# Key gathers cut in four and value loads in two, with seven instead of six score groups ahead of the next exponent pass

## The chip, the cores and the metric

The kernel runs on one core of a Trainium2 chip, in one launch. The metric is the device time in microseconds. Three runs of the kernel before gave 947.57, 948.26 and 948.73 us; the median is 948.26 us.

## The reference, cut to what matters

The reference is a two-layer perceiver block on a sequence of 128 queries of width 256. Each layer is a cross attention to a context of 12544 rows, a second mixer (a gated delta net in layer 0, a linear attention with decay in layer 1) and a mixture of experts. The change touches only the cross attention of layer 1:

```
q = (layernorm(x) @ Wq.T + bq).reshape(128, 16 heads, 16)      # 128 queries
k = (ctx @ Wk.T + bk).reshape(12544, 16 heads, 16)
v = (ctx @ Wv.T + bv).reshape(12544, 16 heads, 16)
scores = einsum('qhd,khd->hqk', q, k) / 4
out = einsum('hqk,khd->qhd', softmax(scores), v)               # the mask is all ones
x = x + out
```

## The kernel before, in words

The context is walked in 14 chunks (NCH) of 896 columns (CH), a chunk being 7 tiles of 128. Layer 0's attention is computed first, and in its passes over the chunks the kernel also makes layer 1's keys (split in three bf16 terms, laid out as 96 rows per head) and values, and stores them in DRAM: `kscr[0]` holds the first 512 columns of each chunk, `kscr[1]` the other 384, and `vscr` the values. Between the layers stand the delta net and the first mixture of experts. From about 549 us on, layer 1's attention reads all of that back.

**The loads.** `gather(sp, c, half)` (L1595) issues one DMA of 96 rows: 16 KB a row for half 0 (1536 KB), 12 KB a row for half 1 (1152 KB). `fetch_values(sp, c)` (L1601) issues one DMA of 128 rows of 8036 bytes (1004.5 KB). Both go into rings of three buffers (R1 = 3) and all are issued by SyncE, in the order of `second_sync` (L1692): in each turn of its loop half 1's gather for chunk c+2, the values of c+2, the three small DMAs of `rows(c+1)` (L1697) and half 0's gather for c+3. After the first turn this reads, in time: `rows(c+1)`, then gathers of half 0 and half 1 of chunk c+3 back to back, then the values.

**The online softmax.** A chunk is worked on twice. First come the maxima: for each head h, "S h" of the plan is one pair of matmuls (`score`, L1810, matmuls at L1818: 128x512 and 128x384) into one of two pairs of PSUM banks, and one VectorE reduction over 896 columns (`largest`, L1974). A pair of banks is free again when the reduction two places before has read it. After S15 VectorE updates the running maximum (L1989), GpSimd turns it into three bf16 terms (`maximum`, L1747: L1750 to L1762), TensorE transposes them ("M", L1826), ScalarE copies them out (L2026), and `rows` moves them by DMA into three rows of the tile `home` (`qrows`), so that the next score matmuls yield the score minus the maximum. The second pass over the chunk has 28 units: TensorE's transposed scores for four heads and one tile (`scores`, L1861, four matmuls, in pairs of units: "x8"), ScalarE's exponent of 128x512 (L2035), and TensorE's product with the values (`values`, L1874, 16 matmuls a unit, four units in a row: the profile shows "x32" pieces with the weights' passes). "R" (L1835, L1994) turns a finished chunk's output and adds it.

**The order.** The order of all engines is written out by hand. Unit groups of the second pass run in 7 x 3 slots (t = 0 to 6, k = 0 to 2): slots k = 0 and 1 hold two score units each, slot k = 2 holds the four value units of the tile. After each slot come the entries of `PLAN1[t][k]` (L1656). `SPLIT = 6` says that S0 to S5 of the plan belong to chunk c+2 and S6 to S15 to chunk c+1. `PRO1` is what is done ahead of the first unit: all S of chunk 0, S0 to S2 of chunk 1, M of chunk 0, then S3 to S5 of chunk 1. TensorE executes strictly in this order. "Chunk c" below means the turn in which the second pass of chunk c is done; one such turn is called a period.

**The waits that matter.** `score` waits at h = 0 for the chunk's two gathers (L1815). `turn_maximum` waits for GpSimd's last term. `scores` waits at u = 0 for `rows` (L1854). `score` also waits, by `sm_free` (L1798), for the reduction two places before.

Of the kernel before, what the change touches and what calls it, by code (L numbers as in the profile page):

```python
# [20 lines left out]
ALU = mybir.AluOpType  # L21
# [7 lines left out]
CT = 7  # L29
CH = CT * P  # L30
HT = (4, 3)
# [10 lines left out]
S0 = D0 ** -0.5  # L42
H1, D1 = 16, 16
# [5 lines left out]
KROWS = NJ * D1  # L49
# [17 lines left out]
def build(nc, a, out):  # L67
# [4 lines left out]
    def S(name):  # L72

        if name not in sems:
            sems[name] = nc.alloc_semaphore(name)
        return sems[name]
# [11 lines left out]
    def some(value):  # L88

        return not (isinstance(value, int) and value <= 0)  # L90
# [24 lines left out]
    with ctx:  # L115
# [14 lines left out]
        half = sb(keep, "half", [P, 2])  # L130
# [128 lines left out]
        kscr = [nc.dram_tensor(f"kscr{half}", (NCH, NJ, P, DC, HW[half]), BF16).ap() for half in range(2)]  # L259
        vscr = nc.dram_tensor("vscr", (NCH, P, CT, VW), F32).ap()  # L260
# [589 lines left out]
        R = sb(gd, "R", [P, NH, P])  # L850
# [9 lines left out]
        w = sq  # L860
# [731 lines left out]
        pickhome = v1[:, 2].rearrange("p t w -> p (t w)")[:, 0:3 * HB * KROWS // 2]  # L1592
        picks = pickhome.bitcast(BF16).rearrange("p (l k r) -> p l k r", l=HB, k=3)

        def gather(sp, c, half):  # L1595

            sp.dma_start(krows[half][0:KROWS, c % R1].rearrange("r h m -> r (h m)"),
                         kscr[half][c].rearrange("j (d h) b m -> (j d) (h b m)", d=D1)
                         ).then_inc(S(f"krows{half}_{c % R1}"), 16)

        def fetch_values(sp, c):  # L1601

            sp.dma_start(v1[:, c % R1].rearrange("p t w -> p (t w)"),
                         vscr[c].rearrange("p t w -> p (t w)")).then_inc(S(f"v1_{c % R1}"), 16)

        def l1_loads(sp):
            o = (0, 6, 8, 10)
# [19 lines left out]
        def value_ones(pool, r):  # L1627
# [21 lines left out]
        LB = (6, 7, 0, 1, 2)  # L1649
        UNITS = CT * H1 // GH  # L1650
        SLOTS = 3
        SPLIT = 6

        PLAN1 = (  # L1656
            (("S6",), ("S7",), ("R",)),
            (("S8",), ("S9",), ("S10",)),
            (("S11",), ("S12",), ("S13",)),
            (("S14",), ("S15",), ("S0",)),  # L1660
            (("S1",), ("M",), ("S2",)),
            (("S3",), ("S4",), ()),
            (("S5",), (), ()))

        def plan1(c, t, k):

# [79 lines left out]
        def second_gpsimd(pool):  # L1746
            def maximum(c):  # L1747
                s = c % 2
                pool.wait_ge(S("run1"), c + 1)
                pool.tensor_scalar(neg1[:], run1[:, s], -1.0, None, ALU.mult).then_inc(S("maxstep1"), 1)  # L1750
                if some(c):
                    pool.wait_ge(S("mt1"), c)
                pool.tensor_scalar(n31[:, 0, 0:H1], run1[:, s], -1.0, None, ALU.mult).then_inc(S("maxstep1"), 1)
                if some(c - 1):
                    pool.wait_ge(S("f1"), c - 1)
                pool.tensor_tensor(dm1[:, s], run1[:, 1 - s], run1[:, s], ALU.subtract).then_inc(S("dm1"), 1)
                pool.wait_ge(S("maxstep1"), 4 * c + 2)
                pool.tensor_tensor(neg1[:], neg1[:], n31[:, 0, 0:H1], ALU.subtract).then_inc(S("maxstep1"), 1)
                pool.wait_ge(S("maxstep1"), 4 * c + 3)
                pool.tensor_copy(n31[:, 1, 0:H1], neg1[:]).then_inc(S("maxstep1"), 1)  # L1760
                pool.wait_ge(S("maxstep1"), 4 * c + 4)
                pool.tensor_tensor(n31[:, 2, 0:H1], neg1[:], n31[:, 1, 0:H1], ALU.subtract).then_inc(S("n31"), 1)  # L1762

            def rescale(c):
                pool.wait_ge(S("acc1"), 2 * c + 1)
                pool.wait_ge(S("f1"), c + 1)
                pool.tensor_tensor(acc1[:], acc1[:], bc(f1[:, c % 2, :], 2, [P, H1, D1 + 1]), ALU.mult).then_inc(S("acc1"), 1)

            def block_mask():
                pool.memset(blk16[:], 1.0).then_inc(S("blk16"), 1)  # L1770
                pool.wait_ge(S("blk16"), nth("blk16"))
                v = blk16[:].rearrange("p (b u) -> p b u", u=DL)
                pool.affine_select(out=v, in_=v, compare_op=ALU.is_ge, fill=0.0, base=0,
                                              pattern=[[-DL, P // DL], [0, DL]], channel_multiplier=1).then_inc(S("blk16"), 1)
                pool.wait_ge(S("blk16"), nth("blk16"))
                pool.affine_select(out=v, in_=v, compare_op=ALU.is_ge, fill=0.0, base=DL - 1,
                                              pattern=[[DL, P // DL], [0, DL]], channel_multiplier=-1).then_inc(S("blk16"), 1)

            make_picks(pool)
            ln_pool(pool, "ln2")  # L1780
            pool.wait_ge(S("qpick_psum"), NPICK)
            value_ones(pool, 2)
            pool.wait_ge(S("v1late_ones"), 4)
            pool.wait_ge(S("q3"), 3)
            for half in range(2):
                pool.memset(krows[half][KROWS:KONES].rearrange("p s h m -> p (s h m)").bitcast(F32),  # L1786
                            TWO_ONES).then_inc(S("krows_ones"), 1)
                pool.wait_ge(S("krows_ones"), half + 1)
            for c in range(NCH):
                maximum(c)  # L1790
                if c:
                    rescale(c - 1)
                else:
                    block_mask()
            rescale(NCH - 1)

        def second_tensor(pe):
# [12 lines left out]
            def score(c, h):  # L1810

                r, b = c % R1, sm_bank(("S", c, h))
                if h == 0:
                    for half in range(2):
                        pe.wait_ge(S(f"krows{half}_{r}"), 16 * (c // R1 + 1))  # L1815
                sm_free(("S", c, h))
                for half in range(2):
                    ins = pe.matmul(bank[b + half][:, 0:HW[half]], qrows[0:KROWS, 0, h, :],  # L1818
                                    krows[half][0:KROWS, r, krow(h), :], start=True, stop=True)
                ins.then_inc(S("sm1"), 1)  # L1820
# [44 lines left out]
            def values(c, u):  # L1865
                t, j, g = u // 4, u % 4, UNITS * c + u
                pe.wait_ge(S("exp1"), g + 1)
                if u == 0:
                    if some(c):
                        pe.wait_ge(S("ots1"), c)  # L1870
                    pe.wait_ge(S(f"v1_{c % R1}"), 16 * (c // R1 + 1))
                for i in range(GH):
                    h = GH * j + i
                    ins = pe.matmul(bank[OT1][32 * i:32 * i + 32, j * P:(j + 1) * P],  # L1874
                                    v1[:, c % R1, t, h * (D1 + 1):h * (D1 + 1) + 32],
                                    p1[:, g % PR, i * P:(i + 1) * P],
                                    start=(u == 0), stop=(t == CT - 1), skip_group_check=True)
                ins.then_inc(S("pv1"), 1)
# [403 lines left out]
```

## Time and profile before

| what | value |
|---|---|
| median of three runs | 948.26 us |
| the profiled execution's own time | 944.76 us |
| its span (first to last instruction) | 943.0 us |
| TensorE busy | 899.3 us, 95% of the span |
| VectorE, ScalarE, GpSimd busy | 704.8, 487.5 and 300.1 us |
| granted TensorE clock, mean | 0.989 |
| layer 1's attention, second pass over 14 chunks | about 596.5 to 906 us |

The profiled execution lies 3.5 us under the median of the timed runs (0.37%), so only differences are carried from one to the other. The rows further down come from the profile page of this execution and from questions put to its trace; times in them are microseconds from the start of the span.

### The profile page before, as it was taken

To read this page: it belongs to the slowest core of one execution; us is meant where nothing else is said; L and a number is where in the kernel's file an instruction comes from. 1 tells how busy PE (TensorE), PEld (TensorE's weight loads), DVE (VectorE), ACT (ScalarE), POOL (GpSimd) and SP (SyncE) were. 2 spreads that over 40 slices of the span, in tenths; PEclk is the share of its full clock that TensorE was granted. 3 is DMA by queue.
4 is the path that set the end of the run, shared out by engine and by line. 5 is a ranking of instruction groups with operands and counts; after the bars stand their busy time and mean duration, and the time that the engine had idled before them with its cause. 6 is when DMAs were issued, how large, how long until landed. Compare 5 with 4: busy or idle time off the path is not lost. (4 is left out here: it accounts for less than half of the span.)

```text
span 943.0 us, 21457 instructions
## 1 busy us (share of the span) xinstructions
PE 899.3 (95%) x8230; PEld 580.0 (62%) x8230; DVE 704.8 (75%) x1216; ACT 487.5 (52%) x1156; POOL 300.1 (32%) x435
## 2 busy tenths in 40 slices
PE   8999999999999999999999989989999999999987
PEld 5444554455445545567788856666667666776675
DVE  3499888988898889997577448768778788887426
ACT  2543454345434544344583413556667666666742
POOL 5564346434643464445065127201100000000100
PEclk9999999999999999999999979999999999999999
DMA  9467855575356535533300078786666667766000
GB/s 171 171 185 211 250 183 171 143 186 183 104 143 186 180 103 158 132 117 119 134 1 1 1 186 215 203 210 163 163 164 164 163 176 185 177 180 187 5 3 6
DMA packets 103655, 136.33 MB, mean 145 GB/s; under 512 B 64152, under 2 KB 85424, under 8 KB 100880
## 3 DMA queue, kind: packets, MB, share of 16 engines
q1 hardware_dynamic: 99856, 134.22, 52.3%
q10 hardware_dynamic: 3712, 0.92, 0.6%
q8 instruction: 59, 0.97, 0.4%
q14 instruction: 28, 0.23, 0.1%
HBM read 81.48 MB, written 53.07 MB: 143 GB/s over the span
## 5 line engine op out<-in xcount | busy, mean ns | idle before, releaser
L1974 DVE TENSOR_REDUCE mx<-bank 128x1 f32<-128x896 f32 x224 | 232.9, 1086 | 54.6 <-PE bank L1818 53.1
L2035 ACT ACTIVATE p<-bank 128x512 f32<-128x512 f32 x392 | 202.9, 602 | 103.7 <-PE bank L1861 103.4
L704 DVE STREAM_TRANSPOSE ew<-sc 32x896 f32<-32x896 f32 x208 | 229.3, 1102 | 15.3 <-ACT sc L788 7.7
L563 PE MATMUL bank<-Wv,ctxT 128*128 128x512 f32 (+1 forms) x336 | 146.4, 575 | 0.0
L1861 PE MATMUL bank<-home,krows 99*128 99x128 bf16 x1568 | 124.7, 220 | 7.7 <-issue 3.4
L1861 PEld LDWEIGHTS bank<-home,krows 99*128 99x128 bf16 x1568 | 101.3, 98 | 46.4 <-issue 9.9
L1818 PE MATMUL bank<-krows,home 96*128 96x512 bf16 x448 | 123.0, 355 | 1.7 <-DMA krows<-kscr 0.9
L1874 PE MATMUL bank<-p,v 128*32 128x128 f32 x3136 | 108.0, 276 | 3.2 <-issue 3.1
L563 PEld LDWEIGHTS bank<-Wv,ctxT 128*128 128x128 f32 x336 | 63.6, 190 | 71.6 <-issue 64.1
L1874 PEld LDWEIGHTS bank<-p,v 128*32 128x32 f32 x3136 | 80.8, 110 | 31.3 <-ACT p L2035 23.0
L445 POOL CAST kt<-kf 128x512 bf16<-128x512 f32 (+1 forms) x56 | 31.3, 558 | 203.3 <-ACT kf L760 203.3
L1750 POOL TENSOR_SCALAR neg<-run 128x16 f32<-128x16 f32 x14 | 3.6, 256 | 264.8 <-DVE run L1989 264.7
L543 PE MATMUL bank<-ctxT,WTk 128*128 128x512 f32 (+1 forms) x192 | 82.5, 552 | 0.7 <-ACT WTq L752 0.7
L760 ACT ACTIVATE kf<-bank,b 128x512 f32<-128x512 f32 (+1 forms) x56 | 35.5, 635 | 87.6 <-PE bank L543 86.5
L527 PE MATMUL bank<-ctxT,Wk 128*128 128x448 f32 x192 | 76.9, 545 | 1.3 <-DVE ctxT L317 1.3
L788 ACT ACTIVATE sc<-sc,neg 128x448 f32<-128x448 f32 x112 | 74.4, 667 | 0.0
L651 DVE CUSTOM_DVE_ANT_0 sc<-bank,pen 128x448 f32<-128x448 f32 x112 | 63.9, 621 | 4.8 <-issue 4.6
L775 ACT COPY v<-bank 128x256 f32<-128x256 f32 x77 | 28.7, 373 | 66.9 <-PE bank L563 66.9
L748 ACT COPY kT<-bank 128x448 f32<-128x448 f32 x56 | 29.8, 532 | 61.9 <-PE bank L527 61.9
L543 PEld LDWEIGHTS bank<-ctxT,WTk 128*128 128x128 f32 x192 | 34.5, 189 | 44.4 <-issue 37.0
L451 POOL TENSOR_TENSOR kt<-kf,kt 128x512 bf16<-128x512 f32 (+1 forms) x56 | 58.2, 1039 | 4.4
L447 POOL TENSOR_TENSOR kt<-kf,kt 128x512 bf16<-128x512 f32 (+1 forms) x56 | 58.0, 1036 | 4.5
(317 smaller groups left out, 1158.1 us busy)
## 6 DMA issues: line engine op xcount, KB each, us to landing
krows<-kscr SPq DMA_DIRECT2D x14, 1536.0 KB, 9.9
krows<-kscr SPq DMA_DIRECT2D x14, 1152.0 KB, 14.7
v<-vscr SPq DMA_DIRECT2D x14, 1004.5 KB, 13.8
vscr<-vpair SPq DMA_DIRECT2D x12, 1004.5 KB, 4.0
kscr<-kt SPq DMA_DIRECT2D x14, 768.0 KB, 3.6
kscr<-kt SPq DMA_DIRECT2D x14, 576.0 KB, 5.1
kscr<-kt SPq DMA_DIRECT2D x14, 512.0 KB, 4.5
ctxB<-ctx SPq DMA_DIRECT2D x56, 112.0 KB, 4.0
```

Source lines behind the costliest of these rows:

```text
L451: pool.tensor_tensor(kh[:, 2, b], f, kh[:, 1, b], ALU.subtract).then_inc(S("k31"), 1)
L527: ins = pe.matmul(bank[kv_bank(op, s)][:, 0:HCH], Wk0[:, i, b * P:(b + 1) * P], turned_context(c)[:, i, half * HCH:(half + 1) * HCH], star ...
L543: ins = pe.matmul(bank[kv_bank(op, s)][:, 0:HW[half]], WTk[:, i, b * P:(b + 1) * P], turned_context(c)[:, i, HO[half]:HO[half] + HW[half]] ...
L563: ins = pe.matmul(bank[kv_bank(op, s)][:, 0:w * D], turned_context(c)[:, i, k * P:(k + 1) * P], Wv01[:, i, 0:w].rearrange("p w o -> p (w o)"),
L651: dve.tensor_tensor_reduce(out=sc0[:, s, h, half * HCH:(half + 1) * HCH], in0=bank[SX[k % 4]][:, 0:HCH], in1=pen0[:, half * HCH:(half + 1) ...
L704: dve.transpose(pT0[j * SQ:(j + 1) * SQ, :, :, i * SQ:(i + 1) * SQ].rearrange("m t h q -> m h t q"), rows[:, j]).then_inc(S("turn0"), 1)
L788: act.activation(sc0[:, s, h, cols], sc0[:, s, h, cols], ACT.Exp, bias=neg0[:, h:h + 1], accum_out=den0[:, s, h, half:half + 1]).then_inc( ...
L1818: ins = pe.matmul(bank[b + half][:, 0:HW[half]], qrows[0:KROWS, 0, h, :], krows[half][0:KROWS, r, krow(h), :], start=True, stop=True)
L1861: ins = pe.matmul(bank[ST1[g % 3]][:, i * P:(i + 1) * P], krows[half][:, c % R1, krow(h), cols], qrows[:, c % 2, h, :], start=True, stop=True)
L1874: ins = pe.matmul(bank[OT1][32 * i:32 * i + 32, j * P:(j + 1) * P], v1[:, c % R1, t, h * (D1 + 1):h * (D1 + 1) + 32], p1[:, g % PR, i * P: ...
L1974: dve.tensor_reduce(mx1[:, c % 2, h:h + 1], psum[:, b:b + 2, :].rearrange("p b n -> p (b n)")[:, 0:CH], AX.X, ALU.max).then_inc(S("smread1 ...
L2035: act.activation(p1[:, g % PR, :], bank[ST1[g % 3]][:], ACT.Exp).then_inc(S("exp1"), 1)
```

## The change

It has four parts.

1. `gather` issues four DMAs in place of one, each for a quarter of the row's 16 head blocks: 4 KB a row for half 0, 3 KB for half 1. All count on the same semaphore, and `score` waits for all four (16 * GPARTS).
2. `fetch_values` issues two DMAs in place of one: tiles 0 to 3 (4592 bytes a row) and 4 to 6 (3444 bytes). `values` waits for both.
3. `SPLIT` is 7, and `PLAN1` is shifted by one: S6 moves from the first slot of a chunk to slot k = 1 of its last tile (there for chunk c+2), every later S moves up one place, and the slot behind the value units of tile 3 becomes empty. `PRO1` gains one S of chunk 1.
4. In `maximum` GpSimd's subtraction `dm1`, which the rescaling factor needs, moves behind the three steps that M waits for.

```diff
+        GPARTS = 4
+
         def gather(sp, c, half):
-            sp.dma_start(krows[half][0:KROWS, c % R1].rearrange("r h m -> r (h m)"),
-                         kscr[half][c].rearrange("j (d h) b m -> (j d) (h b m)", d=D1)
-                         ).then_inc(S(f"krows{half}_{c % R1}"), 16)
+            for part in range(GPARTS):
+                heads = slice(part * H1 // GPARTS, (part + 1) * H1 // GPARTS)
+                sp.dma_start(krows[half][0:KROWS, c % R1, heads].rearrange("r h m -> r (h m)"),
+                             kscr[half][c].rearrange("j (d h) b m -> (j d) (h b) m", d=D1)[:, heads].rearrange("r h m -> r (h m)")
+                             ).then_inc(S(f"krows{half}_{c % R1}"), 16)
 
         def fetch_values(sp, c):
-            sp.dma_start(v1[:, c % R1].rearrange("p t w -> p (t w)"),
-                         vscr[c].rearrange("p t w -> p (t w)")).then_inc(S(f"v1_{c % R1}"), 16)
+            for tiles in (slice(0, HT[0]), slice(HT[0], CT)):
+                sp.dma_start(v1[:, c % R1, tiles].rearrange("p t w -> p (t w)"),
+                             vscr[c, :, tiles].rearrange("p t w -> p (t w)")).then_inc(S(f"v1_{c % R1}"), 16)
...
-        SPLIT = 6
+        SPLIT = 7
         PLAN1 = (
-            (("S6",), ("S7",), ("R",)),
-            (("S8",), ("S9",), ("S10",)),
-            (("S11",), ("S12",), ("S13",)),
-            (("S14",), ("S15",), ("S0",)),
+            (("S7",), ("S8",), ("R",)),
+            (("S9",), ("S10",), ("S11",)),
+            (("S12",), ("S13",), ("S14",)),
+            (("S15",), ("S0",), ()),
             (("S1",), ("M",), ("S2",)),
             (("S3",), ("S4",), ()),
-            (("S5",), (), ()))
+            (("S5",), ("S6",), ()))
...
                 pool.tensor_scalar(n31[:, 0, 0:H1], run1[:, s], -1.0, None, ALU.mult).then_inc(S("maxstep1"), 1)
-                if some(c - 1):
-                    pool.wait_ge(S("f1"), c - 1)
-                pool.tensor_tensor(dm1[:, s], run1[:, 1 - s], run1[:, s], ALU.subtract).then_inc(S("dm1"), 1)
...
                 pool.tensor_tensor(n31[:, 2, 0:H1], neg1[:], n31[:, 1, 0:H1], ALU.subtract).then_inc(S("n31"), 1)
+                if some(c - 1):
+                    pool.wait_ge(S("f1"), c - 1)
+                pool.tensor_tensor(dm1[:, s], run1[:, 1 - s], run1[:, s], ALU.subtract).then_inc(S("dm1"), 1)
...
-                        pe.wait_ge(S(f"krows{half}_{r}"), 16 * (c // R1 + 1))
+                        pe.wait_ge(S(f"krows{half}_{r}"), 16 * GPARTS * (c // R1 + 1))
...
-                    pe.wait_ge(S(f"v1_{c % R1}"), 16 * (c // R1 + 1))
+                    pe.wait_ge(S(f"v1_{c % R1}"), 32 * (c // R1 + 1))
```

On TensorE the change moves the S pairs against the other groups. The place is the third and fourth tile of a chunk up to M, in the kernel before: the pair in the fourth and fifth row is S14, the next one S15, the one behind the value group (L1874) S0 of the next but one chunk, then S1.

```order
L1874 MATMUL bank<-p1,v1 32x128 x16
L1861 MATMUL bank<-home,krows1 128x128 x8
L1818 MATMUL bank<-krows0,home 128x512
L1818 MATMUL bank<-krows1,home 128x384
L1874 MATMUL bank<-p1,v1 32x128 x16
L1818 MATMUL bank<-krows0,home 128x512
L1818 MATMUL bank<-krows1,home 128x384
L1861 MATMUL bank<-home,krows1 128x128 x8
L1818 MATMUL bank<-krows0,home 128x512
L1818 MATMUL bank<-krows1,home 128x384
L1861 MATMUL bank<-home,krows1 128x128 x8
L1826 MATMUL bank<-identb,n31 96x128
```

And now (L1823 is the score, L1866 the transposed scores, L1879 the values, L1831 is M), from the same place on:

```order
L1866 MATMUL bank<-home,krows1 128x128 x8
L1823 MATMUL bank<-krows0,home 128x512
L1823 MATMUL bank<-krows1,home 128x384
L1866 MATMUL bank<-home,krows1 128x128 x8
L1823 MATMUL bank<-krows0,home 128x512
L1823 MATMUL bank<-krows1,home 128x384
L1879 MATMUL bank<-p1,v1 32x128 x16
L1866 MATMUL bank<-home,krows1 128x128 x8
L1823 MATMUL bank<-krows0,home 128x512
L1823 MATMUL bank<-krows1,home 128x384
L1866 MATMUL bank<-home,krows1 128x128 x8
L1831 MATMUL bank<-identb,n31 96x128
```

No S pair stands any more behind that value group: the last pair ahead of it, which was S15, is now S0, and S15 is the pair before. On SyncE, one turn of the loop before (`home<-n3T` is `rows`):

```order
L1697 DMA home<-n3T 1x16x128 x3
L1597 DMA krows<-kscr 96x8192
L1597 DMA krows<-kscr 96x6144
L1603 DMA v<-vscr 128x2009
L1697 DMA home<-n3T 1x16x128 x3
```

And one turn now:

```order
L1702 DMA home<-n3T 1x16x128 x3
L1601 DMA krows<-kscr 96x2048 x4
L1601 DMA krows<-kscr 96x1536 x4
L1608 DMA v<-vscr 128x1148
L1608 DMA v<-vscr 128x861
L1702 DMA home<-n3T 1x16x128 x3
```

The order of the three kinds is kept; ten DMAs of the large tiles stand where three stood.

## Rows read from the trace of the kernel before

**Rows 1.** The page: busy us, share of the span, instructions, by engine.

```profile
PE 899.3 (95%) x8230; PEld 580.0 (62%) x8230; DVE 704.8 (75%) x1216; ACT 487.5 (52%) x1156; POOL 300.1 (32%) x435
```

**Rows 2.** Whom TensorE waited for, 597 to 908 us (total, times, longest).

```profile
PE bank L1826 <- POOL n L1762: 3.9, 11, 0.7
PE bank L1861 <- issue: 3.4, 3, 2.4
PE bank L1874 <- issue: 3.1, 3, 1.5
...
PE bank L1861 <- DMA home<-n3T: 1.1, 2, 0.8
```

**Rows 3.** Instructions in time, 791 to 796 us (start, duration, engine, line).

```profile
791.00 0.55 PE L1818 MATMUL bank<-krows,home 96*128 96x512 bf16 x2
...
792.49 0.55 PE L1818 MATMUL bank<-krows,home 96*128 96x512 bf16 x2
...
793.66 0.22 POOL L1756 TENSOR_TENSOR dm<-run 128x16 f32<-128x16 f32 x1
...
794.41 0.22 POOL L1762 TENSOR_TENSOR n<-neg,n 128x16 bf16<-128x16 f32 x1
...
794.68 0.26 PE L1826 MATMUL bank<-identb,n 128*96 128x128 bf16 x1 [0.33 <-POOL n L1762]
...
795.23 0.28 ACT L2026 COPY n3T<-bank 96x128 bf16<-96x128 bf16 x1
...
795.54 1.93 SPq L1697 DMA_DIRECT2D home<-n3T  x3
```

**Rows 4.** The same view, one period on.

```profile
816.30 0.26 PE L1826 MATMUL bank<-identb,n 128*96 128x128 bf16 x1 [0.32 <-POOL n L1762]
```

**Rows 5.** M in all chunks (ns min/median/max, first and last start).

```profile
L1826 PE MATMUL bank<-identb,n x14: 227/257/257, 592.8 to 883.9; 128*96 128x128 bf16 x14
```

**Rows 6.** SyncE in time, 795.5 to 797.6 us.

```profile
797.51 0.59 SPq L1597 DMA_DIRECT2D krows<-kscr  x1
```

**Rows 7.** The page: DMA issues (count, KB, median us from issue to landing).

```profile
krows<-kscr SPq DMA_DIRECT2D x14, 1536.0 KB, 9.9
krows<-kscr SPq DMA_DIRECT2D x14, 1152.0 KB, 14.7
```

**Rows 8.** DMA issues, 774 to 779.4 us (the same columns).

```profile
krows<-kscr SPq DMA_DIRECT2D x1, 1152.0 KB, 13.8
```

**Rows 9.** DMA issues, 730.5 to 731 us.

```profile
krows<-kscr SPq DMA_DIRECT2D x1, 1152.0 KB, 15.2
```

**Rows 10.** Busy time in stretches; last figures clock, DMA share, GB/s.

```profile
777.00:784.00 7.00, 7.00 (x125) 5.46 (x126) 5.00 (x7) 5.07 (x10) 0.00 (x0) 1.00 1.05 246
...
790.00:791.00 1.00, 1.00 (x16) 0.73 (x13) 1.00 (x2) 0.93 (x2) 0.00 (x0) 1.00 1.00 418
```

**Rows 11.** DMA queues, 731 to 738.8 us (packets, MB, share).

```profile
q1 hardware_dynamic: 134, 1.84, 99.3%
```

**Rows 12.** DMA queues, 738.8 to 739 us.

```profile
q8 instruction: 1, 0.02, 37.5%
```

**Rows 13.** TensorE in time, 738.5 to 742.5 us.

```profile
738.96 1.07 PE L1874 MATMUL bank<-p,v 128*32 128x128 f32 x31
741.58 0.30 PE L1874 MATMUL bank<-p,v 128*32 128x128 f32 x1 [1.55 <-issue]
```

**Rows 14.** TensorE in time, the first pass and its start, 566 to 600 us.

```profile
570.24 0.54 PE L1818 MATMUL bank<-krows,home 96*128 96x512 bf16 x2 [0.88 <-DMA krows<-kscr]
...
592.79 0.26 PE L1826 MATMUL bank<-identb,n 128*96 128x128 bf16 x1 [1.11 <-POOL n L1762]
...
596.51 0.83 PE L1861 MATMUL bank<-home,krows 99*128 99x128 bf16 x12
```

**Rows 15.** The boundary of the first two chunks, 606 to 623 us.

```profile
613.58 1.78 SPq L1697 DMA_DIRECT2D home<-n3T  x3
...
619.59 1.01 PE L1861 MATMUL bank<-home,krows 99*128 99x128 bf16 x8 [2.36 <-issue]
```

## The prediction

> **What bounds the kernel now.** I read the page first: TensorE is busy 899.3 of 943.0 us [rows 1], so whatever is gained must be idle time of TensorE or work that stands in its way. The change lies in layer 1's attention alone, so next came the list of whom TensorE waited for between 597 and 908 us [rows 2]. It is short. Eleven waits for GpSimd's last term ahead of M sum to 3.9 us; six waits with the releaser "issue", behind which the profile shows nothing, sum to 6.5 us; two for the small DMAs of `rows` sum to 1.1 us. M is run 14 times from 592.8 to 883.9 us [rows 5], so a period takes (883.9 - 592.8) / 13 = 22.4 us on average, or 22.2 us without the one wait of 2.36 us at the first boundary [rows 15]. A period with no such gap, from M at 794.68 to M at 816.30, takes 21.6 us [rows 3, 4]. It holds one wait of 0.33 us at M, so TensorE's own work in a period is 21.3 us.
>
> **The wait at M.** In time around 794 us [rows 3]: GpSimd's last term starts at 794.41 and M follows at 794.68, 0.33 us later than TensorE could have come. ScalarE copies M out at 795.23 and SyncE issues `rows` at 795.54. Part 3 brings S15 one S place forward, and the reductions go at VectorE's pace of one S place, about 1 us; part 4 takes one GpSimd step of 0.22 us [rows 3] out of the chain. Both together exceed the 0.33 us by far: the wait at M goes in all periods. ScalarE's copy, however, stands behind four exponents in its own order that wait for TensorE's scores, so `rows` is not issued earlier relative to the scores.
>
> **The gaps with "issue".** At 740.03 TensorE stops for 1.55 us in the middle of a value group [rows 13]. The DMA queues give the reason. Queue q8 carries only instructions, in packets of 16 KB. From 731 to 738.8 us there is no such packet, while the gathers' queue keeps the DMA engines 99% busy [rows 11]; then, at 738.8 to 739 us, one appears [rows 12], just when half 0's gather (issued at about 730, median 9.9 us to landing, rows 7) is through, and TensorE goes on 2.6 us after it. I read this as a fetch of TensorE's own instructions that had to stand behind a whole gather. With a quarter of the gather in each DMA, it would stand behind a quarter: the gather's share of each engine is six rows of 16 KB now, about 7 us at 246 GB/s in sum (1573 KB / 246 = 6.4 us, rows 10), and 1.6 us afterwards.
>
> The Trainium skill ("DMA: Bandwidth & Descriptors", section "Queues, rings and completion order") says that a DMA engine alternates between its queues and finishes what it has as one packet before it switches. The trace agrees as far as the late fetch at 738.8 goes; nothing in it shows a fetch beside small transfers.
>
> So parts 1 and 2 may return most of 6.5 - 2.4 = 4.1 us (the 2.36 us gap of rows 15 is another matter, below), and part 3 another 3.9. If nothing else came in, each period would fall to 21.3 us.
>
> **What is late next: the gathers.** Part 3 also moves S0 of chunk c+3 forward, from 792.49 to the place where S15 stood, 791.00 [rows 3]: the value group between them is now behind it. S0 waits for both gathers of its chunk. Those are issued behind `rows`. This closes a loop that has nothing to do with TensorE's load:
> - from the first of `rows` to the issue of the second gather, which follows the first at once: 797.51 + 0.59 - 795.54 = 2.6 us [rows 3, 6];
> - from there to the landing of half 1: median 14.7 us [rows 7], 13.8 in one period and 15.2 in another [rows 8, 9];
> - from S0's new place to the next `rows`: 795.54 - 791.00 = 4.5 us [rows 3].
>
> The sum is 21.8 us (20.9 to 22.3). Before, with S0 at 792.49, the last piece is 3.05 us, the sum is 20.3, and the loop is hidden under 22.2. Afterwards it is longer than TensorE's 21.3 us. So I expect TensorE to wait at S0 for the gathers, and a period to take 21.8 us.
>
> **Do the quarters land sooner or later?** The trace has no such transfer. From above: SyncE issues six more, and if each cost the 0.59 us of one issue [rows 6] in sequence, landing would come 3.5 us later and a period would take 25.3 us. From below: the values alone move at 418 GB/s against the gathers' 246 [rows 10]; the 2688 KB of both (2.75 MB) take 6.6 us at that rate, not 11.2, and then the loop is well under 21.3. I take no change, which is nearest to the rows: the queue is never empty behind the first quarter (393 KB take 1.6 us, an issue takes 0.6), and bytes and rows are the same.
>
> The skill's same page (section "Bandwidth") has a rule against this change: batch DMAs to at least 1 MiB, a transfer of 64 KB being mostly overhead. By its table a transfer of a few hundred KB runs under 78% of peak. No run here shows it; if it bit, the gathers would be the slower rival below.
>
> **The sum**, against the profiled execution's 944.76 us (span 943.0) and carried to the median of 948.26:
> - ten periods whose S0 waits for gathers: 10 x (21.8 - 22.2) = -4.0 us;
> - since a period is the longer of loop and 21.3 us, the periods with an early landing (20.9) do not gain the full amount: +0.5 us;
> - three periods outside the loop (the first, which is held by DMAs, and the last two, for which nothing is fetched), where only the wait at M goes: -3 x 0.33 = -1.0 us, of which the first gives back its part, +0.3, since `rows` at 613.58 lands behind a value fetch whatever TensorE does, and TensorE waits 2.36 us for it [rows 15];
> - the start: one more S of 0.4 us on TensorE between M at 592.79 and the first scores at 596.51, a stretch in which `rows` is under way [rows 14]. It is covered if `rows` is the later; if not it costs 0.4. The last chunks have one S less. I take +0.1 in all. The first gathers are waited for by 0.88 us at 570.24 [rows 14], with the same question as above; no change.
>
> Total -4.1 us: 948.26 - 4.1 = **944.1 us** (a profiled execution near 940.7).
>
> **Rivals.**
> 1. *The gathers get faster in quarters*, by 0.5 us or more. Then TensorE's 21.3 us is the bound: 10 x (21.3 - 22.2) = -9, with the other terms about -9.7, so 938.6 us. For it: 246 GB/s against 418 leaves room. Against: nothing in the trace ties the low rate to the size of a row.
> 2. *The gathers get slower in quarters*, and S0 becomes a wait in every period: slower than before. The place is S0's wait for `krows`; the price is 10 us for each us of later landing, since ten periods are held by the loop; it decides from 0.4 us on (loop 22.2). With 1.0 us, the loop is 22.8, 10 x 0.6 = +6, one more us at the start: 948.26 + 6 + 1 - 0.6 = 954.7 us. For it: more issues and more descriptors in a queue that is already full for 13 us of a period. Against: the queue hides issues.
> 3. *The change does not shorten the fetches*, because a fetch waits for something else than the gather ahead of it. Then 4.1 us of gaps stay; those between `rows` and S0 are hidden in the loop's slack of 0.5 us a period, the rest adds. I put back 2 us and the forecast becomes 946.5, no change that can be told.
> 4. *The gain at M returns at `rows`*: ScalarE's copy isn't earlier, so the first scores of a chunk wait for the small DMAs, 1.1 us in all now [rows 2]. Freed by 0.33 us a period, TensorE comes that much earlier there. But the wait at S0 has then already slowed it; where loop and this wait meet, the later rules. It would give 13 x 0.33 = 4 us back: 948.
>
> **How the numbers follow.** A measurement of this kernel tells a change from none at about 0.2%, 1.9 us: faster means under 946.4, slower over 950.2. The forecast has 0.45, and with its own range of 941.5 to 946.8 nearly all of it is faster (0.41). Rival 1 has 0.18, all faster. Rivals 3 and 4 have 0.20 together, 0.03 of it faster. Rival 2 has 0.17; nearly all is slower. That gives 0.62 faster, 0.22 the same, 0.16 slower. The range from 938.5 to 950.5 takes in the forecast, rivals 1, 3 and 4 and the mild part of 2, and leaves out gathers that land more than 0.6 us later.
>
> **What would show it.** In the trace of the changed kernel: no wait for GpSimd at M; TensorE waits for "DMA krows<-kscr" at the score matmuls in most periods, some 0.3 to 1 us each; the instruction packets of q8 spread through the gathers, and the "issue" gaps, other than the one at about 617 us, gone; M 14 times at a distance near 21.8 us; the last quarter of half 1 landing about 2.6 + 14.7 = 17.3 us behind the first of `rows`. The forecast is wrong if S0 never waits (rival 1, or my loop is shorter than I think), if the "issue" gaps stay at 4 us (rival 3), or if the period is over 22.2 us (rival 2).

## The result, and the profile after

| | before | after |
|---|---|---|
| median of four runs (lowest to highest) | 947.91 us (947.17 to 948.73) | 933.22 us (932.81 to 934.47) |
| the profiled execution | 944.76 us | 932.81 us |
| its span | 943.0 us | 931.1 us |

The ratio is 0.9844 with a 95% interval of 0.9812 to 0.9875: faster, by 14.7 us. The forecast was 944.1 us, and its range ended at 938.5, so it was wrong by 5 us beyond its own range. The direction was right. Between the two profiled executions lie 11.9 us. The runs of the kernel before that were taken beside the experiments further down lie between 940.3 and 951.4 us, with medians of 944.0 to 945.5, so of the 14.7 us about 3 belong to the four runs taken here. The traces account for 11.9.

M divides layer 1's attention in time. Here it is after, as TensorE's group on that line; its answer before is [rows 5]. The columns are the duration in ns (least, median, most) and the first and last start:

```profile
L1831 PE MATMUL bank<-identb,n x14: 221/221/257, 591.7 to 868.8; 128*96 128x128 bf16 x14
```

From these starts, and from the issue of the first gather (549.5 before, 549.3 after), the span divides as follows, in us:

| stretch | before | after | difference |
|---|---|---|---|
| up to the first gather | 549.5 | 549.3 | -0.2 |
| first gather to first M | 43.3 | 42.4 | -0.9 |
| 13 periods, M to M | 291.1 | 277.1 | -14.1 |
| last M to the end | 59.1 | 62.3 | +3.2 |

The second line is the wait of 0.88 us for the first gathers [rows 14]: it is gone. In the third, the first period falls from 19.9 to 19.3 us and the second (the first boundary) from 25.5 to 22.3; the other eleven fall from 22.3 to 21.4 us each on average. The forecast had 21.8. The two rows of this stretch, from first to last M, one of each kernel, say of what kind the gain is. The columns are the stretch, its length, the busy time of TensorE, its weight loads, VectorE, ScalarE and GpSimd, then the granted clock, the DMA share and GB/s. Before:

```profile
592.79:883.92 291.13, 278.09 (x4744) 198.51 (x4744) 228.51 (x242) 189.76 (x387) 24.35 (x94) 0.99 0.66 173
```

After:

```profile
591.72:868.78 277.06, 273.50 (x4744) 195.66 (x4744) 227.76 (x242) 188.65 (x386) 24.82 (x94) 1.00 0.66 182
```

TensorE runs the same 4744 matmuls in both. Its idle time falls from 291.13 - 278.09 = 13.0 us to 277.06 - 273.50 = 3.6 us, by 9.5; and its busy time falls by 4.6 us as well, though no work was taken out. The second number was nowhere in my sum.

The list of TensorE's waits after, from 560 to 900 us (total, times, longest), stands against [rows 2]:

```profile
PE bank L1866 <- DMA home<-n3T: 2.5, 2, 1.6
PE bank L157 <- DVE xn L144: 2.3, 2, 2.0
PE bank L1866 <- ACT p L2040: 2.2, 9, 0.2
PE bank L1831 <- POOL n L1764: 1.1, 1, 1.1
PE bank L1866 <- issue: 1.0, 1, 1.0
PE bank L1879 <- issue: 0.8, 2, 0.6
```

The eleven waits for GpSimd at M, 3.9 us, are all gone; the one of 1.1 us that is left stands ahead of the first period, where the kernel before has it too [rows 14], outside the stretch of [rows 2]. The "issue" gaps fell from 6.5 us to 1.8. The wait at L157, 2.0 us, belongs to what follows the attention; the kernel before has it at 911 us, behind the stretch. The list has no wait at all for "DMA krows<-kscr": the wait that the forecast put in every period does not exist. New is the wait of 1.6 us for `rows`. It lies at the last boundary, and this is TensorE behind it in time:

```profile
874.12 0.84 PE L1866 MATMUL bank<-home,krows 99*128 99x128 bf16 x12 [1.64 <-DMA home<-n3T]
875.20 0.55 PE L1866 MATMUL bank<-home,krows 99*128 99x128 bf16 x4 [0.24 <-ACT p L2040]
875.68 1.94 PE L1879 MATMUL bank<-p,v 128*32 128x128 f32 x32
```

The value group takes 1.94 us where it takes 1.08 elsewhere, since the granted clock falls after the wait (third column from the end):

```profile
874.00:876.00 2.00, 1.64 (x24) 1.26 (x28) 0.00 (x0) 1.45 (x3) 0.00 (x0) 0.83 0.00 0
876.00:878.00 2.00, 2.00 (x37) 1.53 (x30) 0.32 (x1) 0.62 (x2) 0.00 (x0) 0.50 0.00 0
878.00:880.00 2.00, 2.00 (x46) 1.78 (x43) 0.38 (x1) 1.81 (x4) 0.00 (x0) 0.82 0.00 0
```

A clock of 0.50 is 1.2 GHz in place of 2.4. Weighted over the three windows it costs 2 x (0.17 + 0.50 + 0.18) = 1.7 us; with the wait of 1.64 this is the +3.2 of the last stretch. (Both kernels have a second fall of 3.4 us later in it, at 913 us before and at 899 after, behind the wait at L157. It cancels here.)

And this is the boundary around 784 us, in time, after (the kernel before is in [rows 3, 4]):

```profile
780.12 0.54 PE L1823 MATMUL bank<-krows,home 96*128 96x512 bf16 x2
780.59 1.08 PE L1879 MATMUL bank<-p,v 128*32 128x128 f32 x32
781.00 0.17 DVE L1994 TENSOR_TENSOR run<-run,mx 128x16 f32<-128x16 f32 x1
...
782.38 0.22 POOL L1764 TENSOR_TENSOR n<-neg,n 128x16 bf16<-128x16 f32 x1
782.56 0.22 POOL L1767 TENSOR_TENSOR dm<-run 128x16 f32<-128x16 f32 x1
...
782.92 0.22 PE L1831 MATMUL bank<-identb,n 128*96 128x128 bf16 x1
...
784.27 1.78 SPq L1702 DMA_DIRECT2D home<-n3T  x3
```

M starts at 782.92 with no wait, 0.3 us after GpSimd's last term is through. From here on the loop of the prediction can be read again. The eight key gathers are issued back to back; their row in SyncE's queue, then the last of them alone by its window (issued at 789.9; KB, us to landing):

```profile
786.09 4.18 SPq L1601 DMA_DIRECT2D krows<-kscr  x8
```

```profile
krows<-kscr SPq DMA_DIRECT2D x1, 288.0 KB, 10.6
```

It lands at 789.9 + 10.6 = 800.5 us, 16.2 us behind the first of `rows` (forecast: 17.3). S0, which waits for it, comes a period after 780.12:

```profile
801.28 0.54 PE L1823 MATMUL bank<-krows,home 96*128 96x512 bf16 x2
```

It has no wait, and 0.8 us to spare. The loop is 16.2 + (784.27 - 780.12) = 20.4 us where I had 21.8, and TensorE's own work, 21.2 us a period, is the bound. Over the eleven periods that load a chunk's keys the last landing is 15.9 us behind the first of `rows` on average, against 17.3 before. The page gives the median landings per quarter, which answer to [rows 7]:

```profile
krows<-kscr SPq DMA_DIRECT2D x56, 384.0 KB, 6.4
krows<-kscr SPq DMA_DIRECT2D x56, 288.0 KB, 9.0
```

### The profile page after: what moved, and what is told of

It is laid out like the page before. It is cut to its first block and busy times, and to the rows that moved or that the text cites. A ratio compares the mean times of both kernels' runs of the same rounds, so it can differ in the third digit from the quotient of the medians.

```text
span 931.1 us, 21555 instructions
## 1 busy us (share of the span) xinstructions
PE 895.8 (96%) x8230; PEld 578.0 (62%) x8230; DVE 704.0 (76%) x1216; ACT 487.1 (52%) x1156; POOL 300.6 (32%) x435
## 5 line engine op out<-in xcount | busy, mean ns | idle before, releaser
L1866 PE MATMUL bank<-home,krows 99*128 99x128 bf16 x1568 | 124.3, 220 | 6.0 <-DMA home<-n3T 2.5
L1866 PEld LDWEIGHTS bank<-home,krows 99*128 99x128 bf16 x1568 | 100.2, 98 | 44.0 <-issue 7.8
L1823 PE MATMUL bank<-krows,home 96*128 96x512 bf16 x448 | 122.2, 354 | 0.7 <-ACT home L2049 0.3
L1879 PE MATMUL bank<-p,v 128*32 128x128 f32 x3136 | 107.5, 277 | 0.8 <-issue 0.8
L1879 PEld LDWEIGHTS bank<-p,v 128*32 128x32 f32 x3136 | 80.5, 110 | 31.4 <-ACT p L2040 28.0
```

The lines of the kernel that those rows point to most:

```text
L1866: ins = pe.matmul(bank[ST1[g % 3]][:, i * P:(i + 1) * P], krows[half][:, c % R1, krow(h), cols], qrows[:, c % 2, h, :], start=True, stop=True)
```

## The experiments

Each ratio is against runs of the kernel before on the same chip, with its 95% interval. "Gather time" is from the first packet of half 0 to the end of the last packet of half 1, the mean of 12 gathers in one profile: 13.25 us before, 12.20 after.

The first four (one chip, median before 945.2 us) take the change apart.

**e1_gather4**: the kernel before with its key gathers in four, nothing else.

```diff
+            for part in range(GPARTS):                       # GPARTS = 4
+                heads = slice(part * H1 // GPARTS, (part + 1) * H1 // GPARTS)
...
         SPLIT = 6      # PLAN1, the values and GpSimd's order as before
```

> The kernel before with only the key gathers cut in four (order, values and GpSimd's order as before). Theory F (fetch: TensorE's instruction packets of 16 KB no longer stand behind a whole gather): the 'issue' gaps, 4.1 us in the profile of before besides the one at 617 us, go, the waits at M of 0.33 us stay; 941 to 944 us. Theory L (landing: the gathers themselves land sooner and that alone is the gain): nothing waits for the gathers in this order, so no gain; 947 to 948.5 us. Theory P (the gain is the order alone): 947 to 948.5 us too; F against both.

Measured: 934.12 us (933.5 to 935.31), ratio 0.9889 (0.9847 to 0.9931). This edit alone is worth 11 us, as much as the whole change, where theory F had 4 to 7; F is right in kind and too small in size. Its waits, 560 to 900 us:

```profile
PE bank L1830 <- POOL n L1766: 5.3, 13, 1.1
PE bank L1865 <- ACT p L2039: 2.4, 10, 0.2
PE bank L1878 <- issue: 1.4, 3, 0.6
```

M still waits in every period, and the "issue" gaps fell from 6.5 to 1.4 us. The 13 periods take 282.4 us, 8.7 less than before: 3.7 of it at the first boundary (25.5 to 21.8 us), 5.0 in the other twelve. The gather time is 12.47 us. Sooner landings can't be what shortened these periods: in this order S0 waits for a gather once before, the 0.88 us of the first gathers ahead of these periods, and never now. (Of the 10.7 us between the two profiled executions 1.5 lie ahead of the first gather, where nothing was changed: before, the clock falls to 0.50 for 3.4 us at 500 us, and here it doesn't.)

**e2_plan**: the kernel before with `PLAN1`, `PRO1` and `SPLIT` of the change, nothing else.

```diff
-        SPLIT = 6
+        SPLIT = 7      # and PLAN1, PRO1 with it
```

> The kernel before with only the plan shifted and SPLIT = 7 (one transfer per gather, values and GpSimd's order as before). With whole gathers S0 stands 15 us behind their issue: by my loop of 21.8 us a period against 22.2 us the time falls by 3 to 5 us, to 943 to 945, TensorE waits for krows at the score matmuls in several periods, and the issue gaps stay. Theory P: about 934 us.

Measured: 941.31 us (939.25 to 948.61), ratio 0.996 (0.9931 to 0.9989), so 3.9 us. Its waits:

```profile
PE bank L1861 <- DMA home<-n3T: 4.8, 6, 2.2
PE bank L1861 <- issue: 2.7, 2, 1.8
PE bank L1874 <- issue: 2.4, 4, 1.1
PE bank L1861 <- ACT p L2035: 1.9, 8, 0.2
PE bank L1826 <- POOL n L1762: 1.1, 1, 1.1
PE bank L1818 <- DMA krows<-kscr: 1.0, 3, 0.4
```

The time is a little under the 943 to 945 us that were expected. With whole gathers the waits at M go too and most of the "issue" gaps stay (5.1 us). S0 waits for `krows` in three periods of eleven, 1.0 us in all, where the prediction had 0.3 to 1 us in most periods. The wait for `rows` grows from 1.1 to 4.8 us. The periods gain 5.0 us and the tail, last M to the end, loses 4.0.

**e3_gather1**: the changed kernel with `GPARTS = 1`.

> The changed kernel with the gathers whole again (GPARTS = 1). Differs from the plan-only kernel by values in two and the GpSimd order, neither of which is on the loop: 942 to 945 us, with waits at S0 and issue gaps. Had the quarters nothing to do with the gain: 933 us.

Measured: 942.88 us (939.15 to 946.94), ratio 0.998 (0.9958 to 1.0002). Without the quarters next to nothing of the change is left. The waits have come back, at S0 as well:

```profile
PE bank L1866 <- issue: 3.9, 3, 2.1
PE bank L1879 <- issue: 3.3, 4, 1.0
PE bank L1866 <- DMA home<-n3T: 3.2, 4, 1.8
PE bank L1823 <- DMA krows<-kscr: 3.0, 3, 1.5
```

The longest of the last is the one for the first gathers, at 571 us: 1.50 us here, where the changed kernel has none.

**e4_values1**: the changed kernel with each value load in one DMA.

> The changed kernel with the values in one transfer again. Theory F: a value transfer keeps an engine busy for some 2.5 us against 7 us for a gather, so at most one or two fetches are late: 933 to 935 us. If the values mattered as much as the gathers: 937 us or more.

Measured: 933.89 us (933.48 to 935.44), ratio 0.9888 (0.9846 to 0.993); the gather time is 12.35 us. The changed kernel itself has 0.9894 in e12_changed_again, on another chip: no worth of part 2 shows.

The next four (one chip, median before 945.54 us) vary what the parts of a gather are, all in the changed kernel.

**e5_gather2** and **e6_gather8**: `GPARTS = 2` (8 and 6 KB of a row) and `GPARTS = 8` (2 and 1.5 KB).

> The changed kernel with each gather in two transfers (8 KB and 6 KB a row) instead of four. Both theories put it between the changed kernel (933) and the one with whole gathers (943): 935 to 939 us. It gives the scale for the next two.

> The changed kernel with each gather in eight transfers (2 KB and 1.5 KB a row). With quarters TensorE no longer waits for gathers and hardly for fetches, so nothing is left to gain: 932.5 to 934.5 us. SyncE issues 16 gathers of about 0.5 us, 8 us a turn, behind the maximum rows; if the issue binds the landing, S0 waits and the time is 936 or more.

Measured: halves 936.26 us (932.64 to 939.72), ratio 0.9914 (0.9883 to 0.9945); eighths 930.95 us (930.0 to 931.18), ratio 0.9852 (0.9812 to 0.9892). The gather times are 12.52 and 12.07 us. SyncE's sixteen issues a period do no harm. Eighths came in under the 932.5 us at which I had expected nothing more to gain.

**e8_strided2**: two DMAs, each with two quarters of a row that do not adjoin. So the pieces are those of the changed kernel (4 and 3 KB), and the size of a DMA is that of halves.

```diff
+                sp.dma_start(krows[half][0:KROWS, c % R1].rearrange("r (x y h) m -> r x y (h m)", x=2, y=2)[:, :, part],
```

> The changed kernel with two transfers per gather, each of alternate quarters of every row: pieces as short as the quarters' (4 KB and 3 KB), transfers as large as the halves'. If the length of the pieces decides, it equals four transfers (933 us); if the size of the transfer decides, it equals the kernel with two (935 to 939 us).

Measured: 937.63 us (935.79 to 946.06), ratio 0.9935 (0.9906 to 0.9964); gather time 12.91 us. It is like halves and not like quarters, and S0 waits for `krows` five times, 2.7 us in all. The changed kernel was not run on this chip; on two others it gave 933.2 and 934.3. Short pieces alone don't bring the gain. That the size of the whole DMA does is the reading left.

**e7_rows16**: six DMAs of 16 whole rows in place of four of a quarter of all 96 rows.

```diff
+                rws = slice(part * D1, (part + 1) * D1)      # D1 = 16
+                sp.dma_start(krows[half][rws, c % R1].rearrange("r h m -> r (h m)"),
```

> The changed kernel with each gather cut by rows: six transfers of 16 rows, every row whole (16 KB and 12 KB). Each DMA engine gets one row per transfer. Theory F (a fetch waits for the transfer that the engine is at): one row is 1.1 us, shorter than a quarter's six pieces, so the issue gaps are as small as with quarters. Theory L (what counts is how soon the gathers land, and that depends on the length of a row's piece): whole rows land as late as whole gathers, S0 waits. F alone gives 933, L alone 940 or more. If 16 adjacent rows share few ports into the memory, landing is later still, over 950 us.

Measured: 1074.49 us (1070.98 to 1078.31), ratio 1.1365 (1.1305 to 1.1424). The gather time is 22.6 us, and a packet's time is 124 ns per KB, where whole gathers have 69 and quarters 64. Its waits, 590 to 900 us:

```profile
PE bank L1823 <- DMA krows<-kscr: 61.4, 9, 10.4
PE bank L1866 <- issue: 10.6, 3, 6.0
PE bank L1879 <- issue: 5.9, 2, 5.8
```

It failed as a test of size, since it changed the speed of each packet. It shows two things beside that. The loop of the prediction exists, and binds when gathers are late enough: S0 waits up to 10.4 us. And an "issue" gap can be 6 us long when the transfers take longer.

The next three (one chip, median before 944.02 us) look at the rest of the change and at its cost in the tail.

**e9_dm_first**: the changed kernel with GpSimd's `dm1` back in front (part 4 undone).

> The changed kernel with GpSimd's dm1 step back in front of M's three steps. In the changed kernel the last term is ready at 782.60 and TensorE comes to M at 782.92, 0.3 us later; one step of 0.22 us fits in between. So nothing is waited for in the 11 middle periods, and the last one, where M comes as soon as its term is there, loses 0.2: 933 to 934 us, no change to be told.

Measured: 932.41 us (930.0 to 935.47), ratio 0.9879 (0.983 to 0.9929). No difference: M had 0.3 us to spare, and the step takes 0.22.

**e10_tail**: the changed kernel with another plan in the turn of chunk 12 alone, so that `rows` for the last chunk goes out earlier.

```diff
+        PLAN1_LAST = PLAN1[0:2] + (
+            (("S12",), ("S13",), ("S14", "S15")),
+            ((), (), ("M",)),
+            ((), (), ()), ((), (), ()), ((), (), ()))
```

> The changed kernel with another plan for the turn of chunk 12 alone: S14 and S15 both behind the value group of tile 2, M behind that of tile 3. In the changed kernel the last chunk's first scores wait 1.64 us for the maximum rows and TensorE's granted clock is 0.50 right after, which makes the tail from M of chunk 13 to the end 62.3 us against 59.1 before. If that wait is the cause, the rows come some 2 us earlier, both go, and the time falls by 2 to 3 us, to 930.5 to 931.5. If the lower clock comes from something else than this wait, only 1.6 us go.

**e11_tail8**: the same with `GPARTS = 8`.

> The same with each gather in eight transfers, which took the changed kernel from 933.2 to 931.0 us. The two gains are at different places (the fetches and gathers of all periods; the last boundary), so they should add: 928 to 929.5 us.

Measured: 934.99 us (931.71 to 937.07), ratio 0.9884 (0.9838 to 0.993), and 930.99 us (928.91 to 932.75), ratio 0.9846 (0.9801 to 0.9891). Both miss what was expected. In the profile of e10_tail the last wait for `rows` is gone, the clock stays at 1.00, and the tail is 59.4 us in place of 62.3; but M of the last chunk now waits 1.0 us for GpSimd, and the first boundary of this execution took 26.6 us, with this in its midst:

```profile
618.55 0.61 PE L1871 MATMUL bank<-home,krows 99*128 99x128 bf16 x8 [1.88 <-issue]
```

The two tails can't be compared as they stand. M of the last chunk comes 16 matmuls earlier in this plan, so its tail has that much more work; and the second fall of the clock, behind L157, is absent in this execution. From the last M to the last value matmul it takes 23.4 us, against 25.0 in the changed kernel and 23.75 in e12_changed_again, where the wait for `rows` stands but the clock doesn't fall. The wait is gone; no gain in time is shown.

The last two (one chip, five rounds, median before 944.13 us) repeat the changed kernel and eighths side by side. **e12_changed_again**:

> The changed kernel once more, unchanged. If the gain at the first boundary belongs to the change, M of chunk 1 to M of chunk 2 is 22 to 23 us again; if it is chance, it lies anywhere from 22 to 26.5 us and the span with it. Time 932 to 935 us.

**e13_gather8_again**:

> The changed kernel with eight transfers per gather once more, on the same chip as the repeat of the changed kernel. If fetches still wait behind quarters, eight are faster by 1 to 2.5 us; if nothing is left, the two medians agree within 1 us.

Measured: 934.31 us (933.28 to 936.33), ratio 0.9894 (0.9862 to 0.9927), and 931.26 us (930.49 to 935.33), ratio 0.9861 (0.9826 to 0.9896). The changed kernel is 9.8 us faster than before on this chip. Eighths have a lower median by 3 us here, and by 4 us in e11_tail8 against e10_tail, which also share a chip. In both pairs the intervals of the ratios overlap, so some 3 us is the best estimate and not a settled figure. The lowest medians found, 930.95 to 931.26 us, are all with eighths.

**Instruction fetches, counted.** q8's packets are TensorE's instructions, as far as the gaps below show. From the start of the third gather to 22 us behind the start of the last there are 35 of them in every kernel (but e7_rows16). By their start they stand so against the gather that is under way:

| kernel | packets that start in a gather's first 5 us |
|---|---|
| whole: before, e2_plan, e3_gather1 | 1, 2, 0 |
| halves: e5_gather2, e8_strided2 | 2, 3 |
| quarters: after, e1_gather4, e4_values1 | 4, 4, 3 |
| quarters: e9_dm_first, e10_tail, e12_changed_again | 3, 3, 3 |
| eighths: e6_gather8, e11_tail8, e13_gather8_again | 8, 9, 7 |

Before, they start in clusters at 5.2 to 8.5 and 13.6 to 14.7 us, where one of the two DMAs ends, and none starts between 10 and 13.3 us. This is one that is let in early, in the window 637 to 639.9 us after, 2.2 us into a gather:

```profile
q1 hardware_dynamic: 174, 0.53, 73.3%
q8 instruction: 1, 0.02, 2.5%
```

TensorE has no gap there, where before [rows 11 to 13] the fetch waited for half 0's gather and TensorE stopped for 1.55 us.

**The gaps, held against these packets.** The "issue" gaps of over 0.3 us in the 14 profiles besides e7_rows16 are of two kinds. From 625 us on, each one ends 1.3 to 1.7 us behind the end of a q8 packet; their number and sum are

| kernel | gaps, us in all |
|---|---|
| whole: before, e2_plan, e3_gather1 | 5, 4.2; 5, 3.3; 6, 5.1 |
| halves: e5_gather2, e8_strided2 | 1, 0.7; 3, 2.0 |
| quarters: after, e1_gather4, e4_values1 | 1, 0.6; 2, 1.2; 0 |
| quarters: e9_dm_first, e10_tail, e12_changed_again | 1, 0.4; 3, 2.9; 0 |
| eighths: e6_gather8, e11_tail8, e13_gather8_again | 0; 0; 0 |

These are late fetches, and they go as the DMAs get smaller. The gap at the first boundary, 614 to 620 us, is of another kind: it ends from 0.3 to 4.7 us behind the last q8 packet, 0.26 us in the kernel before, and it is there with eighths as well (1.8 to 2.1 us); only e1_gather4 has none.

## Why the prediction was wrong where it was, step by step

**The wait at M goes: right.** 0.33 us in all periods, 3.9 us in all. Part 4 had no share in it (e9_dm_first).

**Fetches stand behind a gather, and quarters let them in: right in kind, too small in size.** I had 4.1 us of "issue" gaps and, since the loop was to bound the period, no term of its own for them in the sum. The visible gaps shrank by 4.7 us. What I missed is TensorE's busy time, which fell by 4.6 us for the same matmuls. Two parts of it can be read. The profile before shows a granted clock of 0.88, 0.50 and 0.76 in the three windows from 618 us on, in which the gap of 2.36 us at the first boundary ends [rows 15]:

```profile
618.00:620.00 2.00, 0.41 (x5) 0.44 (x6) 0.00 (x0) 0.00 (x0) 0.00 (x0) 0.88 1.06 254
620.00:622.00 2.00, 2.00 (x16) 1.48 (x14) 0.62 (x1) 1.28 (x3) 0.00 (x0) 0.50 1.10 246
622.00:624.00 2.00, 2.00 (x43) 1.62 (x42) 0.82 (x2) 0.95 (x3) 0.00 (x0) 0.76 0.89 178
```

That costs 2 x (0.12 + 0.50 + 0.24) = 1.7 us, and no window of the 13 periods after shows it. The second: a period without any gap but the wait at M takes 21.6 us before, 21.3 without its 0.33; after, clean periods take 21.17. The matmul at M itself takes 221 ns after and 255 before [rows 5]. The 0.1 us by which a period with the stop at M costs more than its wait is 1.4 us in 13 periods. The experiments agree: e1_gather4, with small gathers and the stops at M, has 275.1 us of busy time in this stretch, 3.0 less than before, and the new order brings the other 1.6. The last 1.5 of the 4.6 us I can't assign.

**The loop of 21.8 us that was to bound the period: the step that failed.** Its sum was 2.6 + 14.7 + 4.5 us, and two of the terms were too long.

The landing was put at "I take no change, which is nearest to the rows". From the first of `rows` to the last landing, the mean of eleven periods is 17.3 us before, 17.0 and 17.1 in e2_plan and e3_gather1, where the gathers are whole, and 15.9 with the quarters (16.5 in e1_gather4, 15.5 with eighths). The gather time goes the same way: 13.25 us (13.0 without the one of 15.7 at the first boundary), 13.04 and 13.19; then 12.20 and 12.47. So the quarters took about 1.1 us off the 17.3 of the forecast.

The last piece, from S0's new place to the next `rows`, was read as 795.54 - 791.00 = 4.5 us from a period with M's wait of 0.33 us in it, which the forecast itself took away. In every kernel with the new order it is 4.15 us.

The first error alone was enough: 21.8 - 1.1 is under 21.3. But the loop wouldn't have bound with the old landing either. With whole gathers it is 17.0 + 4.15 = 21.2 us, no longer than TensorE's own 21.17, and e2_plan shows it: S0 waits 1.0 us in all, and what holds its periods at 22.0 us is the "issue" gaps and the waits for `rows`. With quarters it is 15.9 + 4.15 = 20.1 us. So the case was rival 1, to which I gave 0.18, with its bound: no wait at S0 and clean periods of 21.17 us. That e2_plan gained 3.9 us, near the forecast's 4.1, is luck: its profile has 5.0 us gained in the periods by another sum than mine, and 4.0 lost in the tail, which I had not in it.

Taking the loop as the bound also hid the fetches, whose 4.1 us I had named and then dropped. Even rival 1's 938.6 us is 5.4 us above the 933.2 measured; that is the first boundary, the busy time and the scatter of the runs before, less the tail.

The rule of the Trainium skill ("DMA: Bandwidth & Descriptors", section "Bandwidth") to batch to at least 1 MiB speaks for the whole gathers; here 384 and 288 KB beat 1536 and 1152 KB by 11 us (e1_gather4), and 192 and 144 KB did no worse than these. The measurement decides.

**The first boundary, +0.3 us, since "held by DMAs": wrong.** It fell from 25.5 to 22.3 us, and in e1_gather4, where only the gathers' size changed, to 21.8. The gap there, which I put down to `rows`, has "issue" behind it and no fetch at the usual distance: it is 2.36 us in [rows 15] and after

```profile
616.55 0.61 PE L1866 MATMUL bank<-home,krows 99*128 99x128 bf16 x8 [1.04 <-issue]
```

The boundary varies from run to run, though. With quarters or eighths it takes 21.6 to 26.6 us in nine profiles, 23.3 on average (24.7 in e6_gather8, 24.6 in e11_tail8, 26.6 in e10_tail); with whole gathers 24.6, 25.5 and 26.3. So only some 2 of the 3.2 us can be expected of the change.

**The first gathers, no change: wrong by 0.9 us.** The wait of 0.88 us went with the earlier landing. With whole gathers it is 1.50 us in e3_gather1 and nothing in e2_plan, so part of it is chance.

**The tail, one S less: wrong by 3 us.** The sum had nothing for it. Rival 4 said that the gain at M comes back at `rows`. It does so at the last boundary, where no further gather and no next chunk's scores give TensorE other work: a wait of 1.64 us and 1.7 us at half clock. In e2_plan this costs 4.0 us. In e12_changed_again the same wait is followed by no fall of the clock, nor does the second one behind L157 come, and the tail takes 59.7 us. So the plan's gain and its loss are about even, which is why the whole change (933.2 and 934.3 us in its two sets of runs) is hardly ahead of e1_gather4 (934.1).

The account of the 11.9 us is then: 9.5 us of idle time and 4.6 of busy time in the 13 periods, 1.1 ahead of them, less 3.2 in the tail. By part: the quarters give about 11 us, the plan 0 to 1 on top of them, and for the values and GpSimd's order no gain shows. The parts don't add: with whole gathers the plan gives 3.9 us (e2_plan).

**Two slips in the working.** Rival 3 puts 2 us back on 944.1, which makes 946.1 and not 946.5. And the sum has TensorE wait 2.36 us for `rows` at 619.59, where [rows 15] says "issue".

**Does the change make the kernel steadier?** Not shown. Kernels with whole gathers range over 8 to 10 us in sets of 7 to 19 runs, and those with quarters or eighths over 1 to 5.5 us in sets of 4 to 6. The four runs of the kernel before in the first table range over 1.6 us, and the standard deviations overlap: 2.4 to 2.9 us for the first, 0.6 to 2.8 for the second.

**What stays open.** Why smaller DMAs land sooner: e8_strided2 excludes the length of the pieces, and no run separates a shorter start or end of each DMA from a better balance between the engines. The packets' own time falls along with the size of the DMA: 69 ns per KB whole, 68 in e8_strided2, 65 in halves, 63 to 65 in quarters, 59 in eighths. What the gap at the first boundary is, and what sets it from run to run. What gives e10_tail's time back; its profiled execution has that boundary of 26.6 us and three late fetches. A kernel with no instruction fetch during a gather was not tried.

## What to carry to other kernels

Gaps of the busiest engine with no releaser ("issue") are worth a look at the queue of instruction packets. Hold the end of each gap against the end of the last packet: if the distance is always the same, here 1.3 to 1.7 us, they are late fetches. Then cut the large transfers, here until one DMA was 140 to 400 KB, and cut them across all rows, never into a few adjacent rows. Take a loop's terms from a period without the waits that the change removes: the 0.33 us in mine was most of the 0.5 by which it stood over TensorE's own work. A term "no change" for an operation that the trace doesn't show deserves a range as wide as its bounds, and where a loop and an engine's own work lie within 0.5 us of each other, either may be the bound.

## What the runs showed of the hardware that was not expected

- The fetch of TensorE's instructions waits behind the data: with whole gathers 0 to 2 of 35 packets start in a gather's first 5 us, with eighths 7 to 9. TensorE resumes 1.3 to 1.7 us behind the end of a late packet. In e7_rows16 an "issue" gap reached 6.0 us.
- The same bytes in smaller DMAs come in sooner: 13.0 to 13.25 us whole, 12.5 in halves, 12.2 to 12.5 in quarters, 12.1 in eighths.
- DMAs of 16 adjacent rows ran at half speed: 124 ns per KB of a packet against 64 in quarters, 22.6 us a gather against 12.2.
- A wait of 1.64 us at the last boundary was followed by some 3.4 us at half clock in one execution, and by none in another with a wait of 1.65 us there (e12_changed_again).
